# Group graph convolutions of a fused four-layer graph stack: touched rows four graphs deep, the other rows normalized on their own

## The reference

```python
GROUPS = [list(range(25)), [0..8], [0, 9..14], [6, 7, 8, 12, 13, 14], [3, 4, 5, 9, 10, 11]]
def _graph_conv(x, adj, W, b):
    A = adj + jnp.eye(n)
    norm_adj = dinv[:, :, None] * A * dinv[:, None, :]      # dinv = rowsum(A) ** -0.5
    support = einsum('bnd,de->bne', x, W)
    return relu(einsum('bnm,bme->bne', norm_adj, support) + b)
for g, idx in enumerate(GROUPS):                             # 128 -> 256 -> 128 features
    h = _graph_conv(x[:, idx], adj[:, idx][:, :, idx], W1[g], b1[g])
    out_g = _graph_conv(h, adj_g, W2[g], b2[g])
    fused = fused.at[:, idx, :].add(softmax(fusion_w)[g] * out_g)
x = _layernorm(x + fused)
```

## Time and profile before

| what | value |
|---|---|
| median of three executions | 1249.65 us (1249.27 to 1251.31) |
| the profiled execution | 1249.63 us |
| its span, first to last instruction | 1247.8 us |
| busy: PE, DVE, ACT, POOL | 1168.4, 983.6, 843.9, 744.7 us |
| mean granted clock of TensorE | 0.967 of full speed |

### The profile page before, as it was taken

The page is one execution under the profiler, slowest core; times in us unless marked ns, Lnnn a source line. Parts: engine busy times, 40 slices in busy tenths (PEclk is TensorE's granted clock), DMA queues, the critical chain, the costliest instruction groups (busy, mean ns, idle before and its releaser), DMA issues.

```text
span 1247.8 us, 22267 instructions
## 1 busy us (share of the span) xinstructions
PE 1168.4 (94%) x6935; PEld 891.1 (71%) x6935; DVE 983.6 (79%) x2542; ACT 843.9 (68%) x1495; POOL 744.7 (60%) x722
## 2 busy tenths in 40 slices
PE   4899994999999999999999999999999999989991
PEld 3899993777777777777777777777777777767871
DVE  3799995678878787878888787888878788848784
ACT  2588884677767677676777777676777767744563
POOL 2699997456656474665656565565746566533554
PEclk8799997999999999999999999999999999989995
DMA  5233321410101010010101001010101000000224
GB/s 149 85 117 103 103 78 34 62 34 1 34 0 34 0 34 17 17 34 0 34 0 34 17 17 34 0 34 0 34 0 34 27 6 13 1 14 15 81 68 134
DMA packets 96388, 47.82 MB, mean 38 GB/s; under 512 B 19659, under 2 KB 92132, under 8 KB 96356
## 3 DMA queue, kind: packets, MB, share of 16 engines
q1 hardware_dynamic: 96356, 47.43, 13.2%
HBM read 28.58 MB, written 8.81 MB: 30 GB/s over the span
## 4 chain that ended last, share of the span: by engine, by line
PE 76%; DVE 15%; issue 3%; POOL 2%; ACT 2%; DVEq 0%; SPq 0%; DMA 0%; POOLq 0%; ACTq 0%
PE psum L1022 18%; PE psum L1027 18%; PE psum L1023 18%; PE psum L1093 8%; DVE st L711 4%; PE psum L1062 3%; PE psum L1058 3%; DVE x L722 2%; PE psum L1148 2%; DVE mv L715 2%; PE psum L1035 2%; DVE ws L821 1%; DVE ws L811 1%; DVE stc L910 1%; DVE x L906 1%
## 5 line engine op out<-in xcount | busy, mean ns | idle before, releaser
L513 POOL TENSOR_TENSOR htl<-ht,hth 128x512 fp32r<-128x512 f32 x160 | 210.4, 1315 | 310.2 <-ACT hth L651 238.7
L519 POOL TENSOR_TENSOR zh<-zw,ht 128x512 f32<-128x512 f32 x160 | 206.7, 1292 | 46.9 <-ACT zw L619 46.8
L1022 PE MATMUL psum<-hth,wh_hi 128*128 128x512 f32 x480 | 204.1, 425 | 0.7 <-ACT hth L644 0.7
L1022 PE MATMUL psum<-pth,wx_hi 128*128 128x512 f32 x480 | 202.8, 422 | 0.0
L634 ACT ACTIVATE rt<-psum,brz 128x512 f32<-128x512 f32 x160 | 110.2, 689 | 120.7 <-PE psum L1027 120.7
L1027 PE MATMUL psum<-htl,wh_hi 128*128 128x512 f32 x480 | 190.4, 397 | 0.2 <-POOL htl L513 0.2
L1023 PE MATMUL psum<-hth,wh_lo 128*128 128x512 f32 x480 | 189.8, 395 | 0.0
L1023 PE MATMUL psum<-pth,wx_lo 128*128 128x512 f32 x480 | 189.4, 395 | 0.0
L869 DVE TENSOR_TENSOR ptl<-psum,pth 128x512 fp32r<-128x512 f32 x160 | 110.3, 689 | 85.7 <-ACT pth L624 85.7
L1027 PE MATMUL psum<-ptl,wx_hi 128*128 128x512 f32 x480 | 165.9, 399 | 0.0
L619 ACT ACTIVATE zw<-psum,brz 128x512 f32<-128x512 f32 x160 | 110.4, 690 | 43.7 <-PE psum L1027 43.7
(11 more groups left out here) (140 smaller groups left out, 2377.5 us busy)
## 6 DMA issues: line engine op xcount, KB each, us to landing
adj<-in_adj_dram SPq DMA_DIRECT2D x32, 256.0 KB, 2.7
x<-in_x_dram SPq DMA_DIRECT2D x32, 256.0 KB, 3.1
x2s<-x SPq DMA_DIRECT2D x32, 256.0 KB, 2.4
adjr<-in_adj_dram SPq DMA_DIRECT2D x32, 256.0 KB, 2.9
out_dram<-yo SPq DMA_DIRECT2D x8, 1024.0 KB, 4.5
v<-in_L_gnn_W_dram SPq DMA_DIRECT2D x2, 640.0 KB, 5.3
x2s<-x SPq DMA_DIRECT2D x8, 100.0 KB
adjr<-x SPq DMA_DIRECT2D x8, 100.0 KB
```

The source lines that it names most:

```text
L513: nc.gpsimd.tensor_tensor(HT_LO[s][:, :], HT[s][:, :], HT_HI[s][:, :].bitcast(F32), ALU.subtract).then_inc(b_htl[s], 1)
L519: nc.gpsimd.tensor_tensor(ZH[s][:, :], ZW[s][:, :], HT[s][:, :], ALU.mult)\
L1022: mm(dst[:, :], w_h[:, col:col + P], h[:, :], start=start, stop=False)
```

## The change

All of it is in part C and its loads.

- **Layout.** The touched rows of four graphs lie on 100 partitions (`QN`), four such quads a chunk, in four buffers `X3Q`. `m2` becomes a block diagonal of four adjacencies (its loads go from 16 to 32). Support is 4 matmuls of 212 columns. The sum comes back with 4 transposes of 100 columns. DVE adds `X3Q` to it into `XQ` (100x512), takes statistics and aggregates of the four quads, POOL the power (4 columns), DVE applies in place, and SP writes four pieces of 25 nodes.
- **The other rows.** Statistics of all 128 rows of a chunk are taken in step k itself from `x2` as part B left it, before the chunk is convolved. They are applied in step k + 1 by ACT (L686 of the new file) and POOL (L559, L562); of `YO` only nodes 25 to 127 are written out. `nmc` (L927) is formed at the start of step k + 1.
- **Banks and order.** Hidden halves are in banks 0, 1 and 6, 7, support and the second product in 2, 3, the W2 product in 4, 5. PE puts the product with `n2` between the hidden halves, and W2 takes the first half for all groups and then the second, with one wait each. On ACT the first four applies stand ahead of `SP_T`. DVE copies three of the `TT` groups, ACT two. The group adds read groups 1 to 4 from a tile of their own, `OA`, and only the third waits for the first two.
- **Steps.** All ten are written out; a chunk is in flight for three.

The core of the diff, where a line of "..." stands for what is left out. All engines and SP:

```diff
+        def run_c(step):
+            for k in range(STEPS_C + 2):
+                step(k, lambda lag: 0 <= k - lag < STEPS_C)
...
-                    for par in range(2):
+                    for par in range(G4):
                         r, c = par * NODES + m0, par * SLOTS + OFFS[g]
-                        sp.dma_start(m2v[r:r + cnt, :, c:c + SIZES[g]], an[g][at:at + cnt, par:B:2, :])\
+                        sp.dma_start(m2v[r:r + cnt, :, c:c + SIZES[g]], an[g][at:at + cnt, par:B:G4, :])\
...
+            for k in range(STEPS_C + 2):
+                if 4 <= k + 2 < STEPS_C:
+                    sp.wait_ge(c_xq, k - 1)
                     load_c(k + 2)
...
+                if k >= 2:
+                    sp.wait_ge(c_yq, k - 1)
+                    for t in range(G4):
+                        sp.dma_start(out_nm[0:NODES, (k - 2) * GC + t:(k - 1) * GC:G4, :],
```

POOL:

```diff
+            def step_c(k, has):
+                if has(1):
...
+                    wait_apart(pool, c_rs, k)
...
+                    nc.gpsimd.tensor_tensor(yo, x3, MVC[:, 2 * c0:2 * c1:2].unsqueeze(2).to_broadcast([P, ON_POOL, D]),
+                                            ALU.subtract).then_inc(c_dev, 1)
...
                     nc.gpsimd.tensor_tensor(yo, yo, RSC[:, c0:c1].unsqueeze(2).to_broadcast([P, ON_POOL, D]),
                                             ALU.mult).then_inc(c_yop, 1)
...
                 if has(2):
...
+                    nc.gpsimd.tensor_tensor(RSQ[0:QN, :], VEQ[0:QN, :], half[0:QN, 0:QUADS], ALU.pow)\
+                      .then_inc(c_rsq, 1)
+                if has(0):
...
+                    rstd(MVC[:, h * GC * 2:(h + 1) * GC * 2], VEC, RSC[:, h * GC:(h + 1) * GC], GC,
+                         c_mv, k + 1, c_ve, c_rs)
```

DVE:

```diff
+            def step_c(k, has):
+                if has(1):
+                    h = (k + 1) % 2
+                    wait_apart(dve, c_rs, k)
+                    nc.vector.scalar_tensor_tensor(NMC[:, h * GC:(h + 1) * GC],
...
+                    nc.vector.tensor_tensor(xq[0:QN, :], bank[0][0:QN, :], X3Q[(k - 2) % 4][0:QN, :], ALU.add)\
+                      .then_inc(c_xq, 1)
...
+                if has(2):
+                    xq = XQ[k % 2]
+                    wait_apart(dve, c_rsq, k - 1)
+                    for i in range(QUADS):
+                        last = nc.vector.tensor_scalar(xq[0:QN, i * D:(i + 1) * D], xq[0:QN, i * D:(i + 1) * D],
...
+                if has(1):
...
+                    dve.wait_ge(c_ro, NG * k)
+                    for done, (n0, cnt, at) in enumerate(ADDS):
+                        if done == ADDS_FREE:
+                            dve.wait_ge(c_add, (k - 1) * len(ADDS) + done)
+                        nc.vector.tensor_tensor(ov[:, :, n0:n0 + cnt], ov[:, :, n0:n0 + cnt],
+                                                oa[:, :, at:at + cnt], ALU.add).then_inc(c_add, 1)
```

PE:

```diff
+                for q in range(QUADS):
+                    c = q % 2 * w4
+                    last = mm(bank[2 + q // 2][:, c:c + w4], X3Q[k % 4][0:QN, q * D:(q + 1) * D],
+                              m2[0:QN, (k * QUADS + q) * w4:(k * QUADS + q + 1) * w4], start=True, stop=True)
...
+                    for q in range(QUADS):
+                        last = nc.tensor.transpose(bank[0][0:QN, q * P:(q + 1) * P], OT[:, q * QN:(q + 1) * QN],
+                                                   ident[:, :])
                     last.then_inc(c_f, 1)
...
                     for c in range(HC):
+                        pe.wait_ge(c_rh[c], k + 1)
                         for g in range(NG):
...
+                            last = mm(by_group(4, g), v2[:, (g * HC + c) * P:(g * HC + c + 1) * P],
```

More of the change, by code:

```diff
@@ L145, in graph_stack_kernel @@
         n2 = sb("n2", [P, B // 2 * 2 * SLOTS])
[L146 to L151, removed]
+        X2S = [sb(f"x2s{s}", [P, G4 * D]) for s in range(2)]
+        ADJR = [sb(f"adjr{s}", [P, G4 * N]) for s in range(2)]
+        X3Q = [X2S[0], X2S[1], ADJR[0], ADJR[1]]
+        assert QUADS * D == G4 * D and N == D
         YB = [sb(f"yb{s}", [P, G4 * D]) for s in range(2)]
@@ L182, in graph_stack_kernel @@
         NMC = sb("nmc", [P, 2 * GC])
+        XQ = [sb(f"xq{i}", [P, QUADS * D]) for i in range(2)]
+        STQ = sb("stq", [P, QUADS * 6])
+        MVQ = sb("mvq", [P, QUADS * 2])
+        VEQ = sb("veq", [P, QUADS])
+        RSQ = sb("rsq", [P, QUADS])
         w_ld_tr = sem("w_ld_tr")
@@ L231, in graph_stack_kernel @@
                                              sem2("b_rs"), sem2("b_x3"))
-        c_ldx = [sem(f"c_ldx{i}") for i in range(2)]
+        c_ldx = [sem(f"c_ldx{i}") for i in range(4)]
         c_s, c_st = sem("c_s"), sem("c_st")
@@ L561, in _ @@
+            run_c(step_c)
         @block.scalar
@@ L674, in step_c @@
                 if has(0):
-                    act.wait_ge(c_s, k + 1)
-                    nc.scalar.activation(SP_T[:, :].rearrange("p (b x) -> p b x", b=2),
-                                         psum[:, 0:2 * 512].rearrange("p (b x) -> p b x", b=2)[:, :, 0:CS // 2],
-                                         ACT.Copy).then_inc(c_st, 1)
+                    act.wait_ge(c_h[0], k + 1)
+                    for g in range(NG):
+                        last = nc.scalar.activation(grp(HID[0], g), by_group(0, g), ACT.Relu,
+                                                    bias=b1T[:, g * HC:g * HC + 1])
@@ L695, in step_c @@
                     act.wait_ge(c_t, k + 1)
-                    nc.scalar.activation(slots(TT[:, :], 0), per_graph(by_group(0, 0), 0), ACT.Copy)\
-                      .then_inc(c_tt, 1)
-                if has(3):
-                    apply_c(k, m, range(ON_ACT // 2, ON_ACT))
+                    for g in TT_ON_ACT:
+                        last = nc.scalar.activation(slots(TT[:, :], g), per_graph(by_group(4, g), g), ACT.Copy)
+                    last.then_inc(c_tt, 1)
             for s in range(2):
@@ L1121, in step_c, with hid @@
                     last.then_inc(c_n, 1)
-                if has(0) and has(1):
-                    support(k, m)
+                def hid(c, lo):
+                    for g in range(NG):
+                        last = mm(by_group(lo, g), v1[:, (g * HC + c) * P:(g * HC + c + 1) * P],
+                                  slots(SP_T[:, :], g), start=True, stop=True)
+                    last.then_inc(c_h[c], 1)
+                if has(0):
+                    pe.wait_ge(c_st, k + 1)
+                    if k == 0:
+                        pe.wait_ge(b_ye[0], ITERS)
+                        pe.wait_ge(b_z[0], ITERS * L)
+                    if has(2):
+                        pe.wait_ge(c_xq, k - 1)
+                    hid(0, 0)
                 if has(1):
@@ L1145, in step_c @@
-                    for g in range(NG):
-                        for c in range(HC):
-                            pe.wait_ge(c_rh[c], NG * k + g + 1)
-                            last = mm(by_group(0, g), v2[:, (g * HC + c) * P:(g * HC + c + 1) * P],
-                                      grp(HID[c], g), start=c == 0, stop=c == HC - 1)
+                            last = mm(by_group(4, g), v2[:, (g * HC + c) * P:(g * HC + c + 1) * P],
+                                      grp(HID[c], g), start=c == 0 and g < 2, stop=c == HC - 1 and g >= NG - 2,
+                                      skip_group_check=True)
```

252 lines of the change are left out of this document (122 added, 130 removed).

## The result

| | median | lowest to highest |
|---|---|---|
| before | 1249.49 us | 1249.27 to 1251.31 |
| after | 1469.24 us | 1468.12 to 1470.03 |

The changed kernel takes 1.176 times the time of the one before (95% interval 1.174 to 1.177), 220 us more. The forecast was 1246.6, its range 1228 to 1254. No case in it came near.

The account below looks back on a forecast made before the run. It took PE to set the step and a chain across all engines the end. From 1249.63 us, start +4.3, half clock +1.6, seven steps +3.7 and end -12.6 gave -3.0, so 1246.6, range 1228 to 1254.

Parts of the forecast that it names:

- At nothing: Loads into m2 and SP's issues: 16 loads more and nine issues a step at 0.8 us each, counted as costing nothing.
- Start, +4.3: Step 0: 16 statistics and aggregates ahead of DVE's hidden relu make it end 4.3 us later, at 1119.4 or 1119.5.
- Half clock, +1.6: Second half of W2 in step 0: after PE stands for 4 us it runs at half clock, 1.6 us more.
- PE 11.7: PE's work in each step after the change, summed over its matmuls and transposes: 11.7 us.
- DVE 11 to 11.5 plus 0.6: DVE's work in each step: 11 to 11.5 us, plus some 0.6 of handovers.
- The block: Steps 3 to 7: DVE's group adds wait for POOL's subtract and multiply, making steps of 15.1 us.
- The circle without the block, 12.55: A step from nmc to the next nmc, if DVE's adds don't wait for POOL: 12.55 us.
- End, -12.6: After the last W2: 21.2 us to the end of the span for 33.8 before, a gain of 12.6.
- Sum: Start, half clock, seven steps and end together: -3.0 us, so 1246.6 us.
- The clock falls in every step: Rival, chance 0.30: PE's clock halves from F to H's first half in every step, 5.9 us more, 1252.5 us.
- Adds escape, nmc is caught: Rival, chance 0.17: the group adds run free of POOL and nmc waits for its multiply; steps of 14.1, 1238.6 us.
- No block of weight: Rival, chance 0.18: POOL doesn't hold up DVE; steps of 12.5 us, 22.4 us less, 1227.2 us.

Follow-up runs that it names:

- a_split: The changed kernel with its write-out of 103 partitions cut into 96 and 7; 1245.68 us, ratio to before 0.9962.
- p3_spt_first: p2_nmc_early with ACT's copies to sp_t and tn put ahead of its first four applies; 1221.94 us, ratio to before 0.9774.
- p2_nmc_early: a_split with nmc formed in its own step, behind the adds and ahead of the TT copies, and POOL's subtract waiting for it; 1223.91 us.
- p1_adds_first: a_split with one wait more: POOL's subtract also waits for the group adds of the step before; 1232.25 us, ratio to before 0.9862.
- p4_start: p3_spt_first with step 0's hidden relu on DVE ahead of its statistics, and ACT's first four applies of step 1 behind the hidden relu; 1223.34 us.
- a_94_9: The changed kernel with its write-out cut into 94 and 9 partitions; 1305.66 us, ratio to before 1.0445.
- a_104: The changed kernel with one row more in its write-out, 104 partitions in one transfer, and the quad stores waiting for it; 1245.09 us.
- b_104_24: The kernel before with its write-out cut into 104 and 24 partitions; 1252.51 us, ratio to before 1.0019.

## Why the prediction was wrong, point by point

**The step that failed** is the one under "At nothing", with the sum that follows it. It listed the DMAs that the change adds (16 loads into `m2`, nine issues a step) and priced SP's issues at 0.8 us each. The write-out of `YO` was taken over from before as a transfer that costs nothing in the steps, since "of `YO` only nodes 25 to 127 are written out" sounds like less. It had no term for how a transfer is spread over the DMA engines. By the runs: one DMA engine, 41 us for 824 KB, eight in a row, +223.6 us in the changed kernel and +242 in the one before. One of the issues priced at 0.8 stood for 33.33 us behind the first of them. I had allowed for "the last output landing late", a matter of the end, and no rival had a late landing hold up the steps: from the third chunk on, ACT and POOL wait for it before they may write into `YO`.

The trace of before could have warned of it without an edit. It has a transfer of few partitions, the load of 25 rows at the side of PE's work. Its DMA view, 1146 to 1152:

```profile
DMA  0000000000030013333332223332300000000000
GB/s 0 0 0 0 0 0 0 0 0 0 0 109 0 0 55 99 106 92 85 102 106 82 82 82 96 102 102 75 89 24 20 21 0 0 0 0 0 0 0 0
```

It runs mostly at 82 to 106 GB/s and a share of 3 tenths, five engines of 16, where the write-out of 128 partitions fills them all. A price by bytes (824 KB for 1 MB) needs a row with the same spread, and 103 had none.

**The other terms**, measured where the write-out is out of the way (a_split; the start and the first step also in the changed kernel):

- *Start, +4.3.* Step 0 ended at 1119.55 for the 1119.4 or 1119.5 forecast, but 0.5 us of that belong to the next term, so some 3.8. Nearly right.
- *Half clock, +1.6.* Right in size: the second half of W2 took 2.34 for half of 3.68, and S behind it 2.82 for 1.60, 1.7 together. Most of it fell on S, which the prediction hadn't named, and so into step 1. The granted clock was 0.58 from 1119.55 to 1122.20.
- *PE 11.7.* S starts 1.44 before T (1.45 forecast), F takes 0.5 from start to start, and p3_spt_first shows 11.7 a step with PE as the bound. Right.
- *DVE 11 to 11.5 plus 0.6.* Its column in p3_spt_first is 70.66 for seven steps, 10.1. Over by 0.9 to 1.4; it didn't decide.
- *The block.* Right as a mechanism, and in size nearly. a_split's steps 1 to 7 take 12.9, 13.0, 14.4, 15.7, 14.3, 14.1 and 15.8: 100.1 for the forecast 102.5, the last five 14.9 each for 15.1. What I had as one outcome is two: in three steps one add is caught (2.9 to 3.0 us for the seven) and in four two are (4.1 to 4.6). Behind two of the three (at 1146.49 and 1190.87) `nmc` is then caught as well, 1.33 us, where the signs that I gave had it short. The power (L492) is a POOL instruction with two SBUF operands too, and it catches nothing: eleven adds of a_split that started while it ran took 0.19 to 0.30 us, as long as the seven with POOL idle. So the rule of the prediction, that an instruction with two SBUF inputs stands for the whole of a POOL instruction that reads SBUF, is borne out for the subtract and the multiply and not for the power. Its words that no row has a group add beside such an instruction overlook the adds in rows 3, which it had itself placed beside the power. Why the power differs is open.
- *The circle without the block, 12.55.* Somewhat too long. The changed kernel has one such round, in step 2, where the write-out holds POOL back and the adds run free. From `nmc` at 1133.84 (shown above) to the next that is 12.1 us. The 11.8 of p2_nmc_early are another circle, with `nmc` moved.
- *End, -12.6.* 20.7 us behind the last W2 for the forecast 21.2. Right.
- *Sum.* 1246.6 forecast, 1245.68 for the kernel whose write-out is spread over 16 engines. The agreement is closer than its parts. In the profiled execution step 0 ends 1.9 us earlier than 1121.1 (4.3 and 1.6 behind 1115.2), the seven steps are 2.4 shorter and the end 0.5, and that execution took 1242.03, the shortest of its six. So 3.7 us of the median are in none of the numbers above.

The round without the block, on DVE in the changed kernel:

```profile
1143.36 1.18 DVE L984 TENSOR_TENSOR ot<-ot,oa 128x144 f32<-128x144 f32 x7
...
1145.92 0.17 DVE L927 SCALAR_TENSOR_TENSOR nmc<-mvc,rsc 128x16 f32<-128x16 f32 x1
```

**The rivals.** "The clock falls in every step": S ran at 2.94 and 2.80 in two of seven steps of a_split, after PE had stood 2.6 and 2.7 us, and not after 2.4 and 2.2; from F to H these two steps take 4.5 us for 3.1. The granted clock of the seven steps is 0.95. The granted clock in these two places is 0.60, and 1.00 in the same place of step 4. So it exists, at 2.7 us of its 5.9. "Adds escape, nmc is caught" as a whole came only when made by hand (p1_adds_first), and then gave 1232 for 1238.6. "No block of weight" at 1227.2 stands 3 us off p2_nmc_early, which took the block away and moved `nmc`. Both sums leave out the 1.6 of the half clock that the main sum has; with it they are about 1240 and 1229.

That the forecast agrees with a_split within 1 us doesn't make it right. The largest term it weighed was 12.6 us, and the one it left out was 224.

## What to carry to other kernels

When an edit changes the number of partitions of a large DMA, look first at its largest divisor up to 16, and cut the transfer or take a row more until it is near 16; the bytes say little. Where a DVE instruction reads two SBUF operands and a long POOL instruction can start beside it, a wait that makes POOL start later can be worth more than it costs (13.4 us here by the medians, 21.8 with `nmc` moved as well). A step whose end is moved earlier gains only if the next instruction in that engine's order isn't the one that waits (p4_start).

## What was not expected of the hardware

- The rate of a transfer by partitions: 338 to 353 GB/s for 128, 41 to 45 for 94, 20 to 24 for 103, and shares of the DMA engines of 0.14 and 0.08 for the last two (windows of a_94_9 and the changed kernel, the latter with another queue's short transfer in it). That is some 22 GB/s for each engine at 1, 2 and 16 of them. With 13 it is less: 211 GB/s from 1134.5 to 1137.5 in a_104, 16 each.
- An issue on SP behind such a transfer stands until it is nearly over, 33.33 us for the first load behind the first write-out, though no semaphore ties the two. So one badly spread DMA also holds the small ones behind it. Why it stands wasn't tried.
- Two DMA issues for a write-out instead of one cost b_104_24 2.6 us. Where these go is open.
- POOL's power, 2.91 us long, doesn't hold up DVE's adds (0.19 to 0.30 us each beside it), and its subtract and multiply of 1.9 us do (up to 1.93).
